# A four-layer gated cross-attention network: norms begun inside the loops before them, fp4 weights quantised inside the expert blocks

## The reference

```python
x = x + jnp.tanh(g_xattn[l]) * attention_l(_layernorm(x), ctx, ...)
x = x + jnp.tanh(g_ffn[l])   * feed_forward_l(_layernorm(x), ...)

def _layernorm(x, axis=-1, eps=1e-05):
    m = jnp.mean(x, axis=axis, keepdims=True)
    v = jnp.var(x, axis=axis, keepdims=True)
    return (x - m) / jnp.sqrt(v + eps)
```

```python
def fp4_quant_dequant(x):
    xb = x.reshape(shape[:-1] + (shape[-1] // 16, 16))
    scale = jnp.maximum(jnp.max(jnp.abs(xb), axis=-1, keepdims=True) / 6.0, 1e-12)
    xn = xb / scale
    idx = jnp.searchsorted(_MID, jnp.abs(xn))   # _GRID: 0, 0.5, 1, 1.5, 2, 3, 4, 6
    return (_GRID[idx] * jnp.sign(xn) * scale).reshape(shape)
fp4_linear = lambda x, w: jnp.einsum('bsk,nk->bsn', fp4_quant_dequant(x), fp4_quant_dequant(w))
```

## Time and profile before

| | |
|---|---|
| three timed runs | 1736.59, 1744.93, 1745.95 (median 1744.93) |
| the profiled execution: its time | 1738.02 |
| its span, first to last instruction | 1736.3 |
| mean granted clock of TensorE | 0.887 of full speed |
| busy share of the span | PE 82%, DVE 75%, ACT 42%, POOL 21% |
| the chain of work that ended last | PE 71%, DVE 20%, ACT 3%, DMA 2%, issue 2% |
| moved by DMA | 147.7 MB, mean 85 GB/s |

### The profile page before, as it was taken

The page is one execution under the profiler, slowest core; times in us unless marked ns, Lnnn a source line. Parts: engine busy times, 40 slices in busy tenths (PEclk is TensorE's granted clock), DMA queues, the critical chain, the costliest instruction groups (busy, mean ns, idle before and its releaser), DMA issues.

```text
span 1736.3 us, 27180 instructions
## 1 busy us (share of the span) xinstructions
PE 1429.2 (82%) x10234; PEld 1329.2 (77%) x10234; DVE 1301.9 (75%) x2433; ACT 734.3 (42%) x1203; POOL 364.7 (21%) x290
## 2 busy tenths in 40 slices
PE   5894997897975799995894138977989999999995
PEld 4793886686965799995793137976878889999995
DVE  5777778778787487773888877987777848888882
ACT  4442341202433277773451312324433226766762
POOL 2231001001000167773000000001000013544532
PEclk8996998898995699998897558988996999999998
DMA  3231100000002477874001000000002027777783
GB/s 131 97 98 65 55 1 1 1 1 10 1 37 91 158 212 228 237 214 90 8 1 56 0 1 1 1 1 10 1 10 89 1 85 242 210 225 222 209 227 73
DMA packets 46675, 147.70 MB, mean 85 GB/s; under 512 B 11427, under 2 KB 24406, under 8 KB 36950
## 3 DMA queue, kind: packets, MB, share of 16 engines
q1 hardware_dynamic: 28918, 122.30, 20.1%
q0 software_dynamic: 17664, 24.13, 8.1%
HBM read 125.96 MB, written 22.54 MB: 86 GB/s over the span
## 4 chain that ended last, share of the span: by engine, by line
PE 71%; DVE 20%; ACT 3%; DMA 2%; issue 2%; POOL 1%; POOLq 1%; SPq 0%; DVEq 0%; ACTq 0%
PE PS L254 48%; PE PS L849 7%; PE PS L810 3%; PE PS L833 3%; PE PS L937 2%; DVE stats L182 2%; PE PS L230 2%; PE PS L1081 1%; PE PS L842 1%; DVE Y L2251 1%; DVE Y L2250 1%; PE PS L1442 1%; DVE FA L2252 1%; DVE Y L2243 1%; DVE FA L2237 1%
## 5 line engine op out<-in xcount | busy, mean ns | idle before, releaser
L254 PE MATMUL PS<-RA 128*128 128x256 f32 (+3 forms) x6456 | 967.5, 310 | 63.5 <-DVE RA L343 15.9
L254 PEld LDWEIGHTS PS<-RA 128*128 128x128 f32 x6456 | 887.8, 196 | 112.7 <-issue 27.2
L1353 POOL DMA_INDIRECT sum_rows<-Y,KT x92 | 164.1, 1784 | 185.7 <-ACT Y L1390 166.8
L1342 POOL DMA_INDIRECT Y<-normed_rows,KT x92 | 116.0, 1261 | 226.6 <-DVE KT L1156 157.8
L218 POOL TENSOR_TENSOR rstd<-vareps,neghalf 128x4 f32<-128x4 f32 x36 | 40.7, 1130 | 561.8 <-DVE vareps L187 453.9
L849 PE MATMUL PS<-VBF,FA 128*128 128x136 f32 x1024 | 135.6, 286 | 5.4 <-ACT FA L631 5.4
L849 PEld LDWEIGHTS PS<-VBF,FA 128*128 128x128 f32 x1024 | 124.1, 191 | 11.3 <-ACT FA L631 7.5
L1421 DVE TENSOR_TENSOR RA<-FA,RA 128x2048 fp32r<-128x2048 f32 x46 | 105.2, 2288 | 20.3 <-ACT RA L1382 20.3
L230 PE MATMUL PS<-ident,FA 128*128 128x128 f32 x160 | 33.5, 379 | 98.1 <-DVE FA L2252 40.7
L1369 ACT ACTIVATE FA<-PS,unit_bias 128x256 f32<-128x256 f32 x184 | 77.4, 476 | 86.7 <-PE PS L254 82.9
L631 ACT ACTIVATE FA<-PS 128x1024 f32<-128x1024 f32 x64 | 65.6, 1026 | 111.7 <-PE PS L810 111.7
(11 more groups left out here) (249 smaller groups left out, 1932.7 us busy)
## 6 DMA issues: line engine op xcount, KB each, us to landing
FA<-in_eup SPq DMA_DIRECT2D x46, 1024.0 KB, 7.4
FA<-in_edown SPq DMA_DIRECT2D x23, 1024.0 KB, 6.3
FA<-in_edown SPq DMA_DIRECT2D x23, 512.0 KB, 3.7
FA<-in_fside SPq DMA_DIRECT2D x16, 512.0 KB, 3.3
sum_rows<-X SPq DMA_DIRECT2D x2, 2048.0 KB, 7.4
normed_rows<-Y SPq DMA_DIRECT2D x2, 2048.0 KB, 7.2
X<-in_x SPq DMA_DIRECT2D x4, 512.0 KB, 9.2
FA<-in_up SPq DMA_DIRECT2D x4, 512.0 KB, 3.8
```

The source lines that it names most:

```text
L254: ins = pe.matmul(dst, stat(a, k), mov(b, k), start=(first and n == 0), stop=(last and n == len(todo) - 1))
L1342: pool.indirect_dma_start(out=rows_in[p][:, t, :], out_offset=None, in_=normed_rows, in_offset=bass.IndirectOffsetOnAxis(ap=source_of[:, R ...
L1353: pool.indirect_dma_start(out=sum_rows, in_=rows_out[p][:, t, :], in_offset=None, compute_op=ALU.add, out_offset=bass.IndirectOffsetOnAxis ...
```

## The change

**Norms begun early.** `Norm` gets three routines for single tiles. `vector_tile` is one BN_STATS for a tile and, at the last tile of a group, its aggregations and variance. `vector_bias` makes minus mean times rstd for a group, one small VectorE operation. `scalar_tile` makes the normed tile as one ScalarE activation (scale and bias per row) into Y. The norms of the gelu, route, fp4 and relu stages and of attention 1 are now objects that exist ahead of all stages. In the slots of each attention VectorE ends with the statistics of the tile before last, for the norm of the stage that follows (`following`), and GpSimd raises to the power as groups come ready. Where that norm is `made_early` (all but the gelu stage's) ScalarE also makes 11 of the 16 tiles in the slots (`EARLY_TILES`), tile n in slot n + 7; the last five are made behind the barrier (`finish_scalar`). The same is done for attention 1 in the last pair of the linear experts; there the 11 tiles come at the end of ScalarE's stream of that stage. The openings lose their statistics and VectorE norms, ScalarE's weight splits change places with its high parts, and only the last group's `vector_bias` is left; `norm_all` becomes `norm_rest`, for the gelu stage alone. Statistics of attentions 2 and 3's own norms stay where they were.

**Loops unrolled.** `slots` no longer has a hardware loop: all attentions are written out.

**fp4 weights.** `WeightsOfFp4` cuts the 4,224 numbers per partition into six pieces of 704. From swiglu block 2 on VectorE quantises a piece in three blocks, behind the block's last low part; blocks 2 to 19 have a part each. Its buffers lie in the unused parts of FA and Y. GpSimd loads each piece behind its gathers and scatters and stores it to DRAM (`done_rows`) when done. VectorE's routine of the gated experts is written out for all blocks. Attention 2 loads all 2.1 MB of quantised weights back in one SyncE transfer as soon as its last group is turned, and the fp4 stage turns them at once. Its rows are normed into Y; the quantiser works there with scratch in FA.

```diff
+                self.bias_ready = shared("ln_bias")
+                self.early = None
+
+            def made_early(self, name):
+                self.early = NG * EARLY[name]
+                return self
+
+            def vector_tile(self, dve, steps, t):
+
+                ins = dve.bn_stats(stats[:, t, :], self.src[:, t:t + 1, :])
+                if t % GT < GT - 1:
+                    return
+                steps(ins)
+                g = t // GT
+                ts = slice(GT * g, GT * (g + 1))
+                for i in range(GT * g, GT * (g + 1)):
+                    ins = dve.bn_aggr(meanvar[:, i, :], stats[:, i, :])
+                steps(ins)
+                ins = dve.tensor_scalar(vareps[:, ts], meanvar[:, ts, 1], EPS, None, ALU.add)
+                if self.rms:
+                    steps(ins)
+                    ins = dve.scalar_tensor_tensor(vareps[:, ts], vareps[:, ts], 1e-8, meanvar[:, ts, 1], ALU.mult, ALU.add)
+                ins.then_inc(self.stats_ready, 1)
+
+            def vector_bias(self, dve, g):
+                ts = slice(GT * g, GT * (g + 1))
+                dve.wait_ge(self.rstd_ready, self.groups + g + 1)
+                dve.scalar_tensor_tensor(minus_mean[:, ts], meanvar[:, ts, 0], -1.0, rstd[:, ts], ALU.mult, ALU.mult
+                                         ).then_inc(self.bias_ready, 1)
+
...
+        class WeightsOfFp4:
...
+                yf = Y[:, :, :].rearrange("p t d -> p (t d)")
+                self.u, self.m = (yf[:, at:at + FI] for at in (2048, 2048 + FI))
+                small_at = 2048 + 2 * FI
+                self.am, self.sc, self.rs = (yf[:, small_at + n * (FI // FB):small_at + (n + 1) * (FI // FB)] for n in range(3))
...
+                    return A["fp4_gate_up"].rearrange("p c d -> p (c d)")[:, n * FI:(n + 1) * FI]
+                return A["fp4_down"][:, n - (self.PIECES - KC), :]
+
+            def load(self, eng, n):
+                if n >= 2:
+                    eng.wait_ge(self.stored, 16 * (n - 1))
+                eng.dma_start(self.x[n % 2], self.source(n)).then_inc(self.piece_in[n % 2], 16)
+
+            def gpsimd(self, pool, block):
+                first = self.FIRST_BLOCK + self.PARTS
+                if block == 0:
+                    self.load(pool, 0)
+                    self.load(pool, 1)
+                n, part = divmod(block - first, self.PARTS)
+                if part == 1 and 0 <= n < self.PIECES:
+                    pool.wait_ge(self.piece_done, n + 1)
+                    pool.dma_start(self.done_rows[:, n, :], self.x[n % 2]).then_inc(self.stored, 16)
+                if part == 2 and 2 <= n + 2 < self.PIECES:
+                    self.load(pool, n + 2)
+
+            def vector(self, dve, steps, block):
+                n, part = divmod(block - self.FIRST_BLOCK, self.PARTS)
+                if not 0 <= n < self.PIECES:
+                    return
+                x = self.x[n % 2]
+                blocks = lambda v: v.rearrange("p (b i) -> p b i", i=FB)
+                of_block = lambda v: v.unsqueeze(2).to_broadcast([P, FI // FB, FB])
+                if part == 0:
+                    dve.wait_ge(self.piece_in[n % 2], 16 * (n // 2 + 1))
+                    steps(dve.tensor_reduce(self.am, blocks(x), AX, ALU.max, apply_absolute_value=True))
+                    dve.tensor_scalar(self.sc, self.am, -1.0 / 6.0, -1e-12, ALU.mult, ALU.min)
+                    more = 1.0 + 2.0 ** -22
+                    steps(dve.tensor_scalar(self.rs, self.am, more / 6.0, more * 1e-12, ALU.mult, ALU.max))
+                    steps(dve.reciprocal(self.rs, self.rs))
+                    steps(dve.tensor_tensor(blocks(self.u), blocks(x), of_block(self.rs), ALU.mult))
+                elif part == 1:
+                    steps(dve.tensor_scalar(self.m.bitcast(U32), self.u.bitcast(U32), 0x7F800000, None, ALU.bitwise_and))
+                    steps(dve.tensor_scalar(self.m, self.m, self.MAGIC, None, ALU.mult))
+                    steps(dve.scalar_tensor_tensor(self.u, self.m, self.MAGIC, self.u, ALU.max, ALU.add))
+                else:
+                    steps(dve.scalar_tensor_tensor(self.u, self.m, self.MAGIC, self.u, ALU.max, ALU.subtract))
+                    dve.tensor_tensor(blocks(x), blocks(self.u), of_block(self.sc), ALU.mult).then_inc(self.piece_done, 1)
+                    dve.wait_ge(self.piece_done, n + 1)
+
+            def prefetch(self, sp, where):
+                sp.wait_ge(self.stored, 16 * self.PIECES)
+                sp.dma_start(where, self.done_rows.rearrange("p n i -> p (n i)")).then_inc(self.prefetched, 16)
...
+        fp4_norm = Norm(TURNS["fp4"], X, Y, *xt_parts).made_early("fp4")
+        relu_norm = Norm(TURNS["relu"], X, Y, *xt_parts, rms=True, scale=norm_weight).made_early("relu")
...
+
+        def finish_scalar(act, norm, part):
+
+            for t in (range(EARLY_TILES, NT - GT), range(NT - GT, NT))[part]:
+                norm.scalar_tile(act, t)
...
+                        weights_of_fp4.prefetch(sp, fview(FP4_AT, weights_of_fp4.PIECES * FI))
...
                         pr = probs[t % BUFS].rearrange("p (h s) -> p h s", s=S2)
                         pool.wait_ge(max_ready, t + 1)
                         pool.tensor_tensor(pr, pr, mx[t % 2].unsqueeze(2).to_broadcast([P, H, S2]), ALU.subtract).then_inc(sub_done, 1)
+                        if t > GT and (t + 1) % GT == 0:
+                            following.pool_rstd(pool, (t + 1) // GT - 2)
+                    following.pool_rstd(pool, NG - 1)
+                else:
+                    following.gpsimd(pool)
...
-                per_slot = 3
-                taken[0] = slots(dve, work, steps, per_slot)
+                    t = slot.first + slot.p
+                    if following.early is not None and t >= 6 and t % GT == 2:
+                        following.vector_bias(dve, (t - 6) // GT)
+                    if t >= 2:
+                        dve.wait_ge(fin_done, T + t - 1)
+                        following.vector_tile(dve, steps, t - 2)
...
@@ -1169,19 +1298,25 @@
 
             def gpsimd(pool):
                 dispatch.gpsimd_constants(pool)
-                norm.gpsimd(pool)
 
             def scalar(act):
...
-                norm_all(dve, norm, lambda: router.vector_weights(dve))
+                norm.vector_bias(dve, NG - 1)
+                router.vector_weights(dve)
+                for g in range(NG):
+                    norm.vector_lo(dve, g)
...
+                    if gated and turn.has(0):
+                        weights_of_fp4.gpsimd(pool, i)
...
+                steps = Steps(dve, dve_steps, taken[0])
+                for i in range(FIRST_TURN, LAST_TURN + 1):
+                    work(Turn(i - i % 2, i % 2))
+                    if 0 <= i < NBLOCKS:
+                        weights_of_fp4.vector(dve, steps, i)
+                taken[0] += steps.n
...
+                        if q == NE // 2 - 1:
+                            if t >= 1:
+                                dve.wait_ge(e_done, n)
+                                attention1_norm.vector_tile(dve, steps, t - 1)
+                            if t % GT == 1 and t >= GT:
+                                attention1_norm.vector_bias(dve, t // GT - 1)
 
...
+                dve.wait_ge(e_done, job_of(NE // 2 - 1, NT))
+                attention1_norm.vector_tile(dve, steps, NT - 1)
...
+                finish_scalar(act, norm, 0)
                 router.scalar_weights(act)
+                norm.scalar(act, 0)
+                norm.scalar(act, 1)
+                finish_scalar(act, norm, 1)
+                norm.scalar(act, 2)
                 split_hi(act, 0)
-                for g in range(NG):
-                    norm.scalar(act, g)
...
-                    dve.wait_ge(*w_in[i])
-                    Quantiser(steps, flat(i)).all()
-                    dve.wait_ge(q_done, i + 1)
+                norm.vector_bias(dve, NG - 1)
+
+                def quantise_xn(g):
+                    dve.wait_ge(norm.xn_ready, norm.groups + g + 1)
+                    Quantiser(steps, Y[:, GT * g:GT * (g + 1), :].rearrange("p t d -> p (t d)"), fview(0, GT * D), fview(GT * D, GT * D)).all()
+
+                quantise_xn(0)
...
+                pe.wait_ge(weights_of_fp4.prefetched, 16)
```

180 lines of the change are left out of this document (99 added, 81 removed).

## The result

The changed kernel took 1695.01 us in the median of four runs (1688.54 to 1697.71), the kernel before 1741.66 beside it: ratio 0.9735, with a 95% interval of 0.9709 to 0.9762. The forecast was 1699 with a range of 1682 to 1717. The profiled execution took 1692.55, 45.5 less than that of the kernel before (1738.02), where the sum of the forecast said 42.6.

A forecast was written before the change was run, and what follows sets the result against it. TensorE was taken to bound the loops, VectorE or waits the stage openings. Gains of 56.0 less losses of 13.4, net 42.6, gave 1695.4 from the profiled execution and 1702.3 by the median; middle 1699 us, range 1682 to 1717.

The forecast's parts named there:

- What bounds: Whole kernel: time can leave the stage openings, at the price of VectorE work in loops where TensorE ends the chain.
- The barrier: End of each of five stages: last statistics and GpSimd's power come ahead of the barrier, 2.3 us later.
- gelu opening: Gelu stage's start: statistics of groups 2 and 3 leave the path, 1.6 us gained.
- attention 1 opening: Attention 1's start: query products begin 5.1 us after the barrier, 2.1 us gained.
- route and relu: Openings of these stages: TensorE bound, group 2 turned sooner; 4.1 us gained in route, 4.2 in relu.
- rival (c): Route and relu openings: TensorE's clock may stay at 2.4 GHz after a shorter pause, 15.6 us, 1683; chance 0.09.
- fp4 opening: fp4 stage's start, VectorE bound: statistics, three weight pieces and four norms leave, 44.0 us gained.
- Swiglu experts: 18 expert blocks: quantising adds 2.2 us each, 1.5 free, block 9.78 instead of 9.07; 12.2 us lost.
- (a): Swiglu blocks: quantising fully hidden, TensorE keeps 9.07 us a block; 1687, chance 0.10.
- (b): Swiglu blocks: quantising fully exposed, 39 us lost instead of 12; 1726, chance 0.08.
- Attention loops: Attentions 1 and 2: aggregating slots overrun, unrolling gives some back; 0.6 us lost in each, 0 in 0 and 3.
- Rival (d): Attentions slip in every slot, 11 us more, 1710; chance 0.17 together with another rival.

The follow-up runs named there:

- experiment 1: The change without its fp4 part: weights loaded and quantised in the fp4 opening again, swiglu experts as before; 1716.39 us, ratio 0.9873 to the kernel before.
- Experiment 4: The change with the last tile's statistics and GpSimd's last power moved behind the barrier of all five stages; 1683.70 us, ratio 0.968 to the kernel before.
- spread: The change with four pieces quantised in swiglu blocks 1 to 20, five parts each, and two behind VectorE's last block; 1693.0 us, ratio 0.9713.
- late_power: Kernel of Experiment 4: the change with last statistics and last power behind the barriers; 1683.70 us.
- best: spread plus late_power, attention 1's output-weight split behind the high parts of groups 0 and 1, last two pieces stored by SyncE; 1672.37 us, ratio 0.9617.
- experiment 2: The kernel before with only the change's fp4 part: pieces quantised in swiglu blocks, loaded back in attention 2; 1717.88 us, ratio 0.9866.
- experiments 3 and 5: 3: the change without the quantiser's arithmetic in the blocks, all loads and stores kept, 1683.16 us, ratio 0.9663; 5: spread.

## Why the prediction was right, and where it was off

**What bounds.** Openings bound by VectorE or by waits, loops by TensorE: right. What was taken out of the openings came off the time, and what was put into the loops beyond their slack came on, with the one exception of experiment 1, where a wait for a load took the place of 4.2 us.

**The barrier**, 2.3 later: measured 2.2 (2.26 against 0.08), released by GpSimd's power as forecast. Experiment 4 gave 1.0 to 2.6 of it back in each of four openings.

**gelu opening**, 1.6: 1.4 and 1.0.

**attention 1 opening.** The start of the queries 5.1 behind the barrier: 5.17. The gain up to them, forecast 2.1, was 2.9 in one execution and 0.6 in the other, because the gelu block ahead, some 230 us long, differs by 2 us between the two. That the forecast lies between them is in part luck. That the queries themselves would run faster (1.8) was not in the term.

**route and relu.** The order of waits was right, the sizes only where the clock was low: spread's 54.84 is 4.4 less than before, where I had 4.1, and relu's 134.54 is 4.3 less, where I had 4.2. The term that was mis-sized is the logits' and turning's duration: I took the earlier trace rows (3.56 for 16 logits) for all, and in the changed kernel the first two took 2.15 and 2.63. In its number this was rival (c), given 0.09 and 15.6 us; it came true by half in route (3.4) and in the relu opening of one execution of two (2.8). In its mechanism (c) was wrong: the clock did not stay up over the shorter pause. It had fallen by 509.8 in the route stage, the first turning was at the lower level (3.68 us for two groups, where late_power has 1.97 for two in attention 1), and the upper level came back at 516.6 and went again at 520.0. The length of the pause does not decide it either: behind 3.3 us the route's logits saw the upper level in the change and not in spread, behind 3.5 us the relu stage's saw it in the second execution of the change and not in the first, and behind 1.1 us the route's saw it in late_power (16 logits in 1.92) and not in best (3.55). The rule of the Trainium skill that I had set beside it (TensorE: Matmul & The Clock Gate, Part 1), that sustained work releases the clock, fits the rise, which came 4.2 us into unbroken work. It does not explain the rest: the clock fell at 520.0 with the work unbroken and the last 32 logits took 6.97 as before, and in spread it stood at 0.50 through 17 us of the same unbroken work from 517.7 on. What decides it is open. My price of the upper level was a mixture too: of the 32 logits in the earlier trace rows, from 294.26 to 298.84, the clock was at its upper level only until 297.0.

**fp4 opening**, 44.0: 44.9. The load of 2.1 MB landed in 7.8 us, half of the 15 that I had put for it uncovered, and cost attention 2's slots nothing (71.98 in experiment 2, which has the load and not the statistics, and 71.97 before). Experiment 2 has the weights' part at 33.8 of 33.7. The norms' part of the term, 10.4 net of the barrier, holds only together with it: alone it is 6.8, for the reason given in experiment 1.

**Swiglu experts**, 12.2: 12.6. The step that carried it, free 1.5 from exactly two waits, is borne out by both waits gone, by three block lengths on one line, and by experiments 3 and 5 from the other side. The price per piece was 6.48 us where I had 6.5. Rivals (a) and (b), all hidden and all exposed, fall. But I had drawn no use from the same number: with 1.5 free a block and 17 us of idle time behind the last one, the 12.6 could be had for nothing.

**Attention loops**, 0.6 each: 0.4. Statistics 0.8 for 1.05, unrolling 0.4 for 0.5. Rival (d) falls; the overrun of an aggregating slot (5.24) is partly made good in the next (4.61).

**The sum.** Forecast by the profiled execution 42.6, measured 45.5. Of the 2.9 between, the clock in the route opening and in the queries gives 3.4 + 1.8, and 1.2 in the relu experts, 0.8 each behind the swiglu experts and in the fp4 stage and 0.6 in attention 0 go the other way; pieces of that size differ between two executions of one kernel. So the sum is nearer than its terms: 7.3 of gains that I had not in it stand against 4.4 of losses, and the median forecast, 1699, was the middle between two values 7 apart.
